# A four-layer tower: 27 of 64 gathered columns by TensorE in the edge stage, and 72 sorted tiles in the last expert layer

## The reference, cut to what matters

```python
# layer 2, feed-forward: gates from a softmax over the edges that end in a node
h = (x_flat @ W_gat).reshape(M, HEADS, NUM_EXPERTS)          # M = 16384, 4 heads, 4 experts
a_src = (h * att_src).sum(-1)
a_dst = (h * att_dst).sum(-1)
e = leaky_relu(a_src[src] + a_dst[dst], negative_slope=0.2)
e_max = segment_max(e, dst)
ee = exp(e - e_max[dst])
denom = segment_sum(ee, dst)
alpha = ee / (denom[dst] + 1e-16)
msg = h[src] * alpha[:, :, None]
agg = segment_sum(msg, dst)                                   # then layer norm, top 2 of 4
...
# layer 3, feed-forward
probs = softmax(einsum('bsd,de->bse', x, gate_w) + gate_b)
top_probs, top_idx = top_k(probs, 2)
dispatch = sum(one_hot(top_idx, 16) * (top_probs / sum(top_probs))[..., None])
hidden = silu(einsum('bsd,edh->bseh', x, w1)) * einsum('bsd,edh->bseh', x, w2)
return einsum('bseo,bse->bso', einsum('bseh,eho->bseo', hidden, w3), dispatch)
```

## Time and profile before

| | us |
|---|---|
| median of 3 runs | 6353.18 |
| lowest and highest | 6348.93, 6354.44 |
| the profiled execution | 6364.2 |
| its span | 6362.5 |
| edge stage, first operation to the next stage's first | 2988.8 to 4854.0 |
| last dense stage (`expe`), first matmul to last addition | 6133.4 to 6357.3 |

### The profile page before, as it was taken

The page is one execution under the profiler, slowest core; times in us unless marked ns, Lnnn a source line. Parts: engine busy times, 40 slices in busy tenths (PEclk is TensorE's granted clock), DMA queues, the critical chain, the costliest instruction groups (busy, mean ns, idle before and its releaser), DMA issues. The chain is left out here.

```text
span 6362.5 us, 107323 instructions
## 1 busy us (share of the span) xinstructions
PE 4930.8 (77%) x39836; PEld 3328.3 (52%) x39903; DVE 4704.8 (74%) x8272; ACT 2457.9 (39%) x4258; POOL 2476.3 (39%) x2492
## 2 busy tenths in 40 slices
PE   6567968886639999995459999999991098977998
PEld 3453236554426666664447777777771035862452
DVE  6887988888778888885347777777773357768667
ACT  4353433333326666662123333333331043222332
POOL 0010020001413333332877777777775602014555
PEclk8788989997769999997779999999995598978999
DMA  0300000111410000001011112111111000030241
GB/s 17 80 6 1 20 23 29 33 29 37 122 31 6 6 8 11 10 8 58 9 31 41 40 41 45 41 40 41 41 41 19 7 1 3 3 67 15 69 112 34
DMA packets 241800, 202.84 MB, mean 32 GB/s; under 512 B 118570, under 2 KB 216275, under 8 KB 239603
## 3 DMA queue, kind: packets, MB, share of 16 engines
q1 hardware_dynamic: 168862, 141.98, 7.7%
q0 software_dynamic: 72528, 54.99, 5.4%
q10 hardware_dynamic: 12, 0.39, 0.0%
HBM read 109.94 MB, written 67.82 MB: 28 GB/s over the span
## 5 line engine op out<-in xcount | busy, mean ns | idle before, releaser
L3396 PE MATMUL edges_bank<-part_room,hot_room 128*128 128x512 f32 x6400 | 1517.1, 400 | 311.2 <-ACT XT L3417 286.2
L3396 PEld LDWEIGHTS edges_bank<-part_room,hot_room 128*128 128x128 f32 x6400 | 1239.5, 194 | 588.8 <-ACT XT L3417 300.5
L3367 POOL DMA_INDIRECT XT<-gat_node_table,edges_idx x1248 | 1282.2, 1027 | 381.3 <-issue 308.9
L3417 ACT COPY XT<-edges_bank 128x512 f32<-128x512 f32 x800 | 460.6, 603 | 644.7 <-PE edges_bank L3396 637.4
L3511 DVE COPY_PREDICATED XT<-edges_tabs_p,XT 128x1280 f32<-128x1280 int32 (+3 forms) x640 | 539.2, 842 | 34.3 <-DVE edges_acc_s L3559 7.1
L1791 ACT ACTIVATE GT<-attc_sc,attc_nm 128x256 f32<-128x256 f32 x1024 | 400.7, 481 | 43.5 <-DVE attc_nm L1857 43.5
L1805 ACT ACTIVATE GT<-attc_sct 128x1024 f32<-128x1024 f32 x256 | 262.6, 1026 | 327.2 <-PE attc_sct L1725 327.0
L1856 DVE TENSOR_REDUCE attc_mx<-attc_sc 128x4 f32<-128x1024 f32 x256 | 313.4, 1224 | 89.1 <-PE attc_sc L1714 88.8
L3493 DVE TENSOR_SCALAR hot_room<-edges_lanes,edges_nodes 128x640 fp32r<-128x640 f16 x640 | 333.9, 582 | 52.3 <-PE edges_bank L3396 43.9
L505 POOL TENSOR_TENSOR X<-H,ln_f_mean 128x1024 f32<-128x1024 f32 x5 | 11.4, 2280 | 914.0 <-DVE ln_f_shift L542 914.0
L1714 PE MATMUL attc_sc<-XT,attc_tT 64*128 64x256 f32 x2048 | 295.5, 407 | 50.7 <-ACT GT L1791 50.7
(11 more groups left out here) (837 smaller groups left out, 10207.2 us busy)
## 6 DMA issues: line engine op xcount, KB each, us to landing
edges_lanes<-gat_places SPq DMA_DIRECT2D x160, 160.0 KB
gat_states<-GT SPq DMA_DIRECT2D x32, 768.0 KB, 3.3
XT<-gat_node_table,edges_idx POOLq DMA_INDIRECT x1248
expert_pairs<-in_L_ffn_W_dram SPq DMA_DIRECT2D x48, 256.0 KB
XT<-XT SPq DMA_DIRECT2D x32, 256.0 KB
XT<-XT SPq DMA_DIRECT2D x64, 128.0 KB
XT<-XT SPq DMA_DIRECT2D x128, 64.0 KB
sorted_in<-stats SPq DMA_DIRECT2D x1, 5056.0 KB, 31.2
```

The costliest lines, as they stand in the source:

```text
L3367: nc.gpsimd.indirect_dma_start(out=rows[:, k, c, :], out_offset=None, in_=q.t_table, in_offset=bass.IndirectOffsetOnAxis(ap=idx[:, k, c:c ...
L3396: m = nc.tensor.matmul(banks[t % BANKS][:], hot[:, (k * GROUPS + j) % 2, b, t, :], parts[:, p, b].rearrange("p u c -> p (u c)"), start=b = ...
L3417: nc.scalar.copy(fetched[:, (k * GROUPS + j) % 2, t].rearrange("p u c -> p (u c)"), banks[t % BANKS][:]).then_inc(fetched_in, 1)
```

## The change

In the edge stage:

- TensorE makes 27 columns of a chunk, in six groups of 5, 4, 5, 4, 5 and 4; GpSimd fetches 37.
- GpSimd's fetches wait for indices and used rows alone.
- The layout of `inp_s` and `acc_s` is turned (row, head, time), `decay` is kept once for all five rows of a head, and the scan of 1300 elements becomes five scans of 260.
- `lanes` has three slots for six groups, so that a group's load waits for the comparisons of the group three before it.
- In ScalarE's `during`, groups 0 to 4 keep their places around the exponentials and copies, and group 5 comes last.

In the last expert layer, 72 tiles are sorted and 56 are dense: `expd` keeps 4 blocks, `expe` has 3 (48 units), `exps` has 87 tiles. The ninth part of 8 tiles is fetched into the second half of XT. `collect.add` of a part stands where its share of the units has passed (`landed`), one unit later.

```diff
-SORTED, SLOTS_TILE, COLLECT = TILES // 2, 2 * P, 8
+SORTED, SLOTS_TILE = 72, 2 * P
+SORTED_PARTS = SORTED // 8
+FIRST_DENSE = (TILES - SORTED) // 16 + 1
...
+                def landed(k):
+                    return (k + 1) * NU // SORTED_PARTS + 1
...
-                    if collect is not None and u and u % COLLECT == 0:
-                        collect.add(v, link, u // COLLECT - 1, target)
+                    if collect is not None and u == landed(parts_added) and u < NU - 1:
+                        collect.add(v, link, parts_added, target)
+                        parts_added += 1
...
-GROUPS, PER_GROUP = 5, 5
-ON_PE = GROUPS * PER_GROUP
+GROUP_SIZES = (5, 4, 5, 4, 5, 4)
+GROUPS, WIDEST = len(GROUP_SIZES), max(GROUP_SIZES)
+GROUP_AT = [sum(GROUP_SIZES[:j]) for j in range(GROUPS)]
+ON_PE = sum(GROUP_SIZES)
...
-    PARTS, BANKS, LANE_SLOTS = 2, 5, GROUPS
+    PARTS, BANKS, LANE_SLOTS = 2, WIDEST, GROUPS // 2
...
-        inp_s, acc_s, decay = (st.sb(n, [P, HEADS2, 1 + PERH, W]) for n in ("inp_s", "acc_s", "decay"))
-        lanes = st.sb("lanes", [P, LANE_SLOTS, PER_GROUP, P], F16)
+        inp_s, acc_s = (st.sb(n, [P, 1 + PERH, HEADS2, W]) for n in ("inp_s", "acc_s"))
+        decay = st.sb("decay", [P, HEADS2, W])
+        lanes = st.sb("lanes", [P, LANE_SLOTS, WIDEST, P], F16)
...
-                        sp.wait_ge(hot_ready, (n - 1) * GROUPS + j + 1)
+                        sp.wait_ge(hot_ready, n * GROUPS + j + 1 - LANE_SLOTS)
...
                     for c in range(BY_DMA):
-                        if c and banks_before is not None:
-                            wait_apart(pool, bank_full, banks_before + c * ON_PE // BY_DMA, passed)
                         nc.gpsimd.indirect_dma_start(
...
-                        v.wait_ge(bank_full, n * ON_PE + (j - 1) * PER_GROUP)
+                        v.wait_ge(bank_full, n * ON_PE + (GROUP_AT[j - 1] if j else -GROUP_SIZES[-1]))
...
-                    nc.scalar.activation(decay[:, :, :, 1:], bc(diff[:, 1], 2, 1 + PERH), ACT.Exp).then_inc(exped, 1)
+                    nc.scalar.activation(decay[:, :, 1:], diff[:, 1], ACT.Exp).then_inc(exped, 1)
...
-                    vec.tensor_tensor_scan(acc_s[:].rearrange("p h j t -> p (h j t)"), decay[:].rearrange("p h j t -> p (h j t)"),
-                                           inp_s[:].rearrange("p h j t -> p (h j t)"), 0.0, ALU.mult, ALU.add).then_inc(sums_ready, 1)
+                    for e in range(1 + PERH):
+                        m = vec.tensor_tensor_scan(acc_s[:, e].rearrange("p h t -> p (h t)"), decay[:].rearrange("p h t -> p (h t)"),
+                                                   inp_s[:, e].rearrange("p h t -> p (h t)"), 0.0, ALU.mult, ALU.add)
+                    m.then_inc(sums_ready, 1)
...
-        experts(nc, g, "expd", tables_d, target=g.H, blocks=4, spread=sort)
+        experts(nc, g, "expd", tables_d, target=g.H, blocks=FIRST_DENSE, spread=sort)
         sorted_experts(nc, g, "exps", sort)
-        experts(nc, g, "expe", tables_d, target=g.H, first_block=4, blocks=4, collect=sort, result=out)
+        experts(nc, g, "expe", tables_d, target=g.H, first_block=FIRST_DENSE, blocks=(TILES - SORTED) // 8 - FIRST_DENSE, collect=sort, result=out)
```

More of the change, by code:

```diff
@@ L780, in tensor @@
         pe.wait_ge(self.split, 1)
-        for c in range(self.tiles // 16):
+        for c in range(-(-self.tiles // 16)):
             if c >= 2:
                 pe.wait_ge(self.moved, c - 1)
-            for m in range(8):
+            for m in range(min(8, self.tiles // 2 - 8 * c)):
                 pair = self.g3[:, 16 * c + 2 * m:16 * c + 2 * m + 2, :].rearrange("p t c -> p (t c)")
@@ L789, in scalar @@
     def scalar(self, act):
-        for c in range(self.tiles // 16):
+        for c in range(-(-self.tiles // 16)):
             act.wait_ge(self.turned, c + 1)
-            self.nc.scalar.copy(self.g.GT[:, c * 8 * P:(c + 1) * 8 * P], self.pt[c % 2][:]).then_inc(self.moved, 1)
+            n = min(8, self.tiles // 2 - 8 * c) * P
+            self.nc.scalar.copy(self.g.GT[:, c * 8 * P:c * 8 * P + n], self.pt[c % 2][:, 0:n]).then_inc(self.moved, 1)
 class ExpertTables:
@@ L859, in __init__ @@
         self.collected = st.sem("collected")
-        self.fetched = [st.sem(f"fetched{k}") for k in range(SORTED // 8)]
+        self.fetched = [st.sem(f"fetched{k}") for k in range(SORTED_PARTS)]
+        whole = self.g.X[:].rearrange("p (t c) d -> p t c d", c=2)
+        rest = self.g.XT[:, TOKENS // 2:TOKENS // 2 + (2 * SORTED - TILES) * D].rearrange("p (t c d) -> p t c d", c=2, d=D)
+        self.back = [whole[:, 8 * k:8 * k + 8] if 16 * k < TILES else rest[:, 8 * k - TILES // 2:8 * k + 8 - TILES // 2]
+                     for k in range(SORTED_PARTS)]
     def sync(self, sp):
@@ L955, in _ @@
                 pe.wait_ge(both_ready, 1)
-                per = PAIRS // 2
+                per = 512 // E
                 for k, m in ((1, all_ones), (0, below)):
-                    for part in range(2):
-                        mm = nc.tensor.matmul(pl[:, k, part * per:(part + 1) * per, :], m[:],
-                                              both[:, part * per:(part + 1) * per, :], start=True, stop=True)
+                    for at in range(0, SORTED, per):
+                        part = slice(at, min(at + per, SORTED))
+                        mm = nc.tensor.matmul(ranks[:, k, part, :], m[:], both[:, part, :], start=True, stop=True)
                     mm.then_inc(ranked, 1)
@@ L3300, in edge_softmax, with last_in_bank @@
         lanes_in = [st.sem(f"lanes_in{j}") for j in range(GROUPS)]
+        def last_in_bank(j, t):
+            before = [(GROUP_AT[m] + t - turn * ON_PE) for turn in (0, 1) for m in range(GROUPS)
+                      if t < GROUP_SIZES[m] and (turn or m < j)]
+            return max(before)
         with nc.Block() as block:
@@ L3410, in _, with take @@
                 act.sem_inc(state_ready, 1)
-                def take(n, j, k, some=range(PER_GROUP)):
+                def take(n, j, k, some=range(WIDEST)):
                     if some[0] == 0:
@@ L3454, in during @@
                     turn_sums(c, k)
-                    take(c + 1, 4, 1 - k, range(2, PER_GROUP))
+                    take(c + 1, 4, 1 - k, range(2, WIDEST))
                     turn_totals(k)
```

82 lines of the change are left out of this document (44 added, 38 removed).

## The result

| | before | with the change |
|---|---|---|
| median (lowest to highest) | 6352.10 us (6348.93 to 6354.44), 4 executions | 6257.94 us (6255.40 to 6269.34), 4 executions |
| ratio, with its 95% interval | | 0.9856 (0.9839 to 0.9873) |
| profiled execution (its span) | 6364.20 (6362.5) | 6256.17 (6254.4) |
| first column of TensorE in the edge stage | 2997.82 | 2992.15 |
| last maxima of the edge stage | 4835.75 | 4747.73 |

The change makes the kernel 94 us faster by the medians; 117 were forecast, so 6257.9 stands against 6236: inside the range of 6208 to 6288, but 3 us above the main case's own 6220 to 6255. Between the two profiled executions it is 108.0, but 5.7 of those came about ahead of the edge stage (2997.82 against 2992.15).

A forecast was written before the change was run, and what follows sets the result against it. GpSimd's fetches, 52.06 us a chunk, were taken to bound the edge stage. Gains of 101 us there and 17 in the last experts, less 1 for rounding, took 6353.2 to 6236, range 6208 to 6288.

The forecast's parts named there:

- main case: Whole kernel: 101 us gained in the edge stage and 17 in the last experts, 6236 us, range 6220 to 6255, chance 0.57.
- The bound: Edge stage: GpSimd's 52.06 us a chunk sets the period before; with 27 columns TensorE's 48.95 exceeds GpSimd's 47.9.
- Fetches and waits for columns: GpSimd, edge stage: two of 39 fetches go, 2.5 us a chunk; removed waits for columns cost nothing.
- Short scans: VectorE's five scans beside GpSimd's fetches, edge stage: stretch of 0.3 us a chunk, bounds 0 and the present 2.2.
- rival (a): Short scans block GpSimd like the long one: 50.05 us a chunk, GpSimd stays the bound, gain 81, 6272 us; chance 0.13.
- The period: Edge stage: 49.4 us a chunk, 0.45 lost where ScalarE is 0.3 short for TensorE's bank; bounds 48.95 and 51.
- rival (b): TensorE stalls briefly each chunk behind ScalarE's copy of sums or late lanes: 50.5 to 51.5, 6268 to 6298; chance 0.16.
- Start and end: Edge stage's ends: TensorE resumes at 3241.4, second fetches land at 3268.2, last maxima start at 4734.6 instead of 4835.75.
- the settling: Start of edge stage: second fetches some 7 us too late for chunk 2; with two chunks of settling, 11 lost.
- Last layer: Last experts: GpSimd becomes the bound, dense stage 32.7 us shorter, sorted stage 13.6 more, routing some 2 more; 17 gained.
- (c): Edge stage: no stall at all, 48.95 us a chunk and faster settling, 101 + 16 with 17, 6215 us; chance 0.07.
- (d): Late lanes, over 5 us behind issue, stall TensorE and lower its clock: 54.75 us a chunk, 6418 us; chance 0.04.

The follow-up runs named there:

- lanes first: The change with SyncE's three loads of columns for the next chunk issued ahead of its wait for used starts and the load of starts; 6225.16 us, ratio 0.9796.
- the single scan and early lanes: The kernel with SyncE's loads of columns issued ahead of the load of starts, with the single scan of 1300 elements back; 6263.67 us, ratio 0.9863.
- the 26 columns: The kernel with SyncE's loads of columns issued first, with 26 columns by TensorE and 38 fetches by GpSimd; 6244.93 us, ratio 0.9834.

## Why the prediction was right, and where it missed

**The bound.** Right: GpSimd's 52.06 us a chunk was the period of before, and with the fetches stretched no more the period fell to 39 x 1.285 in the kernel with short scans alone. TensorE's 48.95 for 27 columns is right to 0.05 (48.92 with lanes first).

**Fetches and waits for columns.** Right: 1.29 a fetch, the waits free in both directions.

**Short scans.** The term was 0.3 us a chunk; the longest fetch between 3400 and 4600 us took 1.41 (that of the chunk shown 1.29), and all fetches beside the scans together are stretched by 0.4 a chunk, where it was 2.1 beside the single scan. GpSimd's need of 47.9 came out at 47.7. Its wait for used rows, 1.5 a chunk forecast, is none until 4030 us and 1.9 a chunk from there. One sum of this part was wrong: 37 x 1.25 + 1.3 + 2.2 is 49.75, and the 50.05 of the upper bound and of rival (a) count the 0.3 as well; with the single scan and early lanes the period was 49.75. The single scan of 2.87 us, all of whose operands lie in SBUF, held fetches of 3.01 and 3.54 us again when it was put back. For the single scan this is what the Trainium skill's "SBUF — State Buffer", section "Who interferes with whom", gives where it lets the second engine block for the whole instruction. Its inferred remark that a tensor_tensor with two SBUF inputs leaves descriptor generation free, which the prediction carried over to scans, does not hold for these scans beside these fetches: the measurement decides against it. A fetch reads its 128 places from SBUF (`edges_idx`), and these rows do not tell for which side of the shared pair it waits. For the short scans the first rule fits only in part: the fetch at 4030.86 was stretched, but the next one, which started at 4032.45, beside the last two scans, took 0.94. Why it passed stays open.

**The period,** 49.4 forecast and 50.20 measured, is the term that was off, and it was named at the right place: TensorE's bank behind ScalarE's copy of the sums. The mis-sized term is the landing of the lanes. I took 2.1 us from the load of starts, which has the same 128 KB; in this trace the comparison begins 3.06 behind the issue (4008.53 to 4011.59), and the 26 columns show that a load of lanes by itself lands in 2.9 to 3.3. The issue itself came when forecast, 0.19 behind the logits' scans and 0.64 later for the lanes. So VectorE waited 2.61 in this chunk and 2.8 on average, not 1.7, and the 0.3 short on ScalarE became 1.2 a chunk, of which the profile shows 0.8 as idle time. Over 28 periods 0.80 makes 22 us. This is the mechanism of rival (b), somewhat below the sizes that I gave it. VectorE's slack, 0.9 forecast, was larger: it still waits 1.6 a chunk for TensorE (39.9 us in 25).

**Start and end.** TensorE resumes 243.3 us behind its first column (243.6 forecast), and the last maxima 7.0 behind TensorE's end (7.3). The second arrival comes 6.9 earlier by the stage's own clock (7.0). With these right, the stage is 101 forecast, less 22 for the period, which leaves 79 where 82 were measured. I put the other 3 down to the settling, 11 us forecast; that is what is left over, and no row measures it.

**Last layer.** 17 forecast, 19 by the traces. GpSimd became the bound of the dense stage as said: 183.8 us for 144 fetches (186.6), VectorE waits for them at some additions, and the stage is 35.4 shorter (32.7). The sorted stage cost 14.7 (13.6).

**The number.** The stage fell 19 us short of its forecast and the last layer brought 2 more: 102 us by the two stages of the traces, where the medians say 94. The other 7 us no stage shows; medians of the kernel before itself differ by 6. The time lies between the main case's own range (to 6255) and that of rival (b) (from 6268), so the whole range holds it because it was made to hold both.

**Rivals.** (a) fell: no fetch in the steady stretch took over 1.45 us, where (a) names fetches of 2 to 3 us as its sign. (c), 48.95 and no stall, is not what the change did, but what it does once SyncE's loads stand in the other order. (d) fell: the lanes landed in 3.1, it needed 5.

## What to carry to other kernels

When a change makes a ring of buffers shorter, look at what stands ahead of each refill in its queue: here three loads behind an unrelated wait cost 33 us, and their order alone gave them back. When several engines are balanced within a few per cent, an edit can leave the period as it is and still pay: an engine that is quicker than the bound builds a lead, and the last chunks spend it. So follow the lead from chunk to chunk and not the period alone, and measure the edit together with the cure of the other bound as well (the single scan cost 14 us in one kernel and 38 in the other). Two loads of equal bytes need not land in equal time: take the duration of the same kind of load.

## What had not been expected of the hardware

A load of 128 KB that spreads one row over all 128 partitions landed 2.9 to 3.3 us behind its issue, with no other load of its queue within 6 us, where one that brings each partition its own rows landed in 2.1 to 2.2. Short stalls of TensorE are larger than its idle time in the profile: 0.8 us of idle time a chunk went with a period 1.2 us longer, at a granted clock of 1.00 in both, since a matmul's record outlasts the next one's start by 0.16. And the time ahead of the edge stage differs by up to 17.4 us between the profiled executions (first column at 2980.45 to 2997.82), with no order in it by what the kernels change, and as much as the part of the last stage; landmarks within a trace told what medians could not.
